# A megakernel's reload of queries and keys: the transfer begun by ScalarE instead of SyncE

## What is computed

```python
h = _L0_tok_ref(x, ln1_g, ln1_b, W, b, ln2_g, ln2_b)      # layernorm, patches @ W + b, layernorm
h = jnp.concatenate([h, txt], axis=1)
h = h + _L0_attn_ref(_layernorm(h), Wq, bq, Wk, bk, Wv, bv, Wo, bo)
h = h + _L0_ffn_ref(_layernorm(h), W_r, W_k, W_v, mu_r, mu_k)

# _L0_attn_ref: heads of 16 features; n, s, e = x.shape
Q, K, V = proj(Wq, bq), proj(Wk, bk), proj(Wv, bv)         # (n, 16, s, 16)
scores = jnp.einsum('nqhd,nkhd->nhqk', Q, K) * scale
out = jnp.einsum('nhql,nlhd->nqhd', softmax(scores), V).reshape(n, s, e)
```

## Time and profile before

| | |
|---|---|
| three timed runs, us | 1626.0, 1631.94, 1637.81 |
| median, us | 1631.94 |
| profiled execution: span from first to last instruction, us | 1635.7 |
| mean granted clock of TensorE | 0.968 of full speed |
| PE busy | 89% of the span |
| ACT busy | 67% |

### The profile page before, as it was taken

One profiled execution on the slowest core, in us unless ns is written; L12 is line 12 of the kernel. 1 busy time (PEld: TensorE's weight loads), 2 busy tenths in 40 slices (PEclk: granted clock), 3 DMA queues, 4 the chain that ended last, 5 costly groups with the idle time before them and its releaser, 6 DMA issues. The chain is left out here.

```text
span 1635.7 us, 53680 instructions
## 1 busy us (share of the span) xinstructions
PE 1454.6 (89%) x18762; PEld 1382.2 (85%) x18762; DVE 1332.3 (81%) x3075; ACT 1099.9 (67%) x2230; POOL 973.6 (60%) x1507
## 2 busy tenths in 40 slices
PE   4678899899999999999999999999999999998856
PEld 4677898898998898889898898998988988897756
DVE  5576888798988989898898888898898988888642
ACT  4455777677777776776777676777777776775543
POOL 2121566567656666666766765675675676576556
PEclk8798999999999999999999999999999999999988
DMA  4279979889877887888887896898898799887651
GB/s 121 59 141 138 141 147 150 125 159 157 143 157 141 147 155 143 150 137 165 149 140 157 151 141 127 167 157 141 152 154 140 151 159 140 156 151 118 131 74 37
DMA packets 702658, 227.65 MB, mean 139 GB/s; under 512 B 617470, under 2 KB 673854, under 8 KB 702394
## 3 DMA queue, kind: packets, MB, share of 16 engines
q1 hardware_dynamic: 702394, 224.23, 77.9%
HBM read 121.64 MB, written 89.64 MB: 129 GB/s over the span
## 5 line engine op out<-in xcount | busy, mean ns | idle before, releaser
L1026 PE MATMUL bank<-wqkv,xnT 128*126 128x384 f32 (+1 forms) x1728 | 354.2, 349 | 5.5 <-issue 5.5
L1118 PE MATMUL bank<-wtok,xT 128*98 128x258 f32 x2304 | 310.2, 290 | 12.0 <-DVE xT L770 11.4
L1026 PEld LDWEIGHTS bank<-wqkv,xnT 128*126 128x126 f32 (+1 forms) x1728 | 294.0, 185 | 18.3 <-issue 10.2
L1118 PEld LDWEIGHTS bank<-wtok,xT 128*98 128x98 f32 x2304 | 294.2, 171 | 14.6 <-DVE xT L770 13.2
L667 POOL TENSOR_TENSOR mixp<-mixf,mixp 128x364 fp32r<-128x364 f32 x192 | 185.2, 976 | 107.2 <-ACT mixp L1000 106.6
L921 ACT ACTIVATE arena<-qk,ymask 128x768 f32<-128x768 f32 x192 | 164.0, 926 | 97.6 <-DMA qk<-qkv_dram 97.6
L843 DVE TENSOR_TENSOR qkvt<-bank,bqkv 126x384 f32<-126x384 f32 (+1 forms) x288 | 154.0, 548 | 48.5 <-PE bank L1026 47.0
L654 POOL TENSOR_TENSOR dT<-zT 128x364 f32<-128x364 f32 x96 | 79.7, 851 | 153.9 <-ACT zT L994 153.9
L609 POOL TENSOR_TENSOR rs<-ve,small 126x3 f32<-126x3 f32 (+1 forms) x160 | 150.3, 940 | 12.5
L607 POOL TENSOR_TENSOR ve<-mv,small 126x3 f32<-126x3 f32 (+1 forms) x160 | 58.8, 368 | 158.8 <-DVE mv L865 104.0
L765 DVE TENSOR_REDUCE xs<-xim 84x14 f32<-84x1792 f32 x64 | 128.7, 2011 | 23.1 <-ACT xim L955 22.8
(11 more groups left out here) (121 smaller groups left out, 3339.6 us busy)
## 6 DMA issues: line engine op xcount, KB each, us to landing
xim<-in_x SPq DMA_DIRECT2D x128, 294.0 KB
qk<-qkv_dram SPq DMA_DIRECT2D x48, 768.0 KB, 8.3
qkv_dram<-qkvt SPq DMA_DIRECT2D x96, 378.0 KB
arena<-qkv_dram SPq DMA_DIRECT2D x384, 48.0 KB, 3.9
qkv_dram<-qkvt SPq DMA_DIRECT2D x48, 336.0 KB
o_dram<-probs SPq DMA_DIRECT2D x288, 48.0 KB, 1.9
out<-h SPq DMA_DIRECT2D x96, 126.0 KB
on<-o_dram SPq DMA_DIRECT2D x64, 126.0 KB
```

Of the source, the lines that this page charges most:

```text
L1026: ins = mm(psum, left(a, k), right(b, k), start=t == 0, stop=t == len(terms) - 1)
L1118: ins = mm(place("tok", c)[0:PT, 0:E + 2], xT[:, a, i0:i0 + GRID // 2, :].rearrange("p i w -> p (i w)"), wtok[:, b, ch, :], start=t == 0, ...
```

## The change

The step `qk_in` leaves SP's program and comes into ACT's, at the same place of the order (15678), ahead of `kspread` in the loop over the steps. Source, target, semaphores and waits are the same.

```diff
@@ SP's program
-                    for k in due(q, s, "qk_in", 0):
-                        after_all(qkv_out, q, k)
-                        after(kb_sb, q, k - 1, 4)
-                        after(q_sb, q, k - 1, 2)
-                        src = qkv_dram[k % CPQ, :, :, 0:2 * HD]
-                        qk_in.done(sp.dma_start(qk[:, :, :], src.rearrange("(g t) i j -> (t i) g j", t=8)))
@@ ACT's program
                     for n in weights_due(q, s):
                         square_weight(n)
+                    for k in due(q, s, "qk_in", 0):
+                        qkv_out.wait(act, q, k)
+                        settle(act)
+                        kb_sb.wait(act, q, k - 1, 4)
+                        settle(act)
+                        q_sb.wait(act, q, k - 1, 2)
+                        src = qkv_dram[k % CPQ, :, :, 0:2 * HD]
+                        qk_in.done(act.dma_start(qk[:, :, :], src.rearrange("(g t) i j -> (t i) g j", t=8)))
                     for yy in range(4):
                         for k in due(q, s, "kspread", yy):
```

## The result

| | before | after |
|---|---|---|
| median of 4 timed runs, us | 1633.84 | 1799.58 |
| lowest to highest, us | 1626.0 to 1637.81 | 1797.34 to 1801.17 |
| profiled span, us | 1635.7 | 1795.3 |
| mean granted clock of TensorE | 0.968 | 0.933 |

The kernel became 10.2% slower, ratio 1.1022 [1.099, 1.1055]. The forecast was 1651 us with a range up to 1696: the sign was right, the size 166 us instead of 19, and the result lies above the range.

A forecast was written before the change was run, and what follows sets the result against it. PE was taken to bound the kernel, busy 1454.6 of 1635.7 us, with at most 43.8 us to win before the scores. Terms of +8, -8 and +19 us gave 1651 us (+1.2%), range 1608 to 1696.

The forecast's parts named there:

- When ACT can issue: At ACT's new place: ACT comes before qkv_out lands and stands 1.1, 2.9, 1.3 us in third, first, second chunk.
- Term 1: ACT's wait delays mixh and xn, costing PE 0.5 us in each quad's third chunk: +8 us, bounds 0 to 32.
- Term 2: Earlier copies in the second chunk remove PE's idle before the scores: -8 us, bounds 0 to -43.8.
- Term 3: On its own queue qk shares DMA engines with xim and v_in; third chunk lands later: +19 us.
- lower end: Third chunk: of 0 to 3.1 us reaching PE, 1.2 was taken, giving 19 us.
- upper end: Third chunk: landing up to 729, with 3.1 us reaching PE, 50 us in place of 19.
- Shared descriptor generator: Rival: ACT and SP share one generator, so ACT's early issue delays o_in: 66 us, 1698 us; chance 0.14.
- Faster: Rival: transfer keeps its speed, ACT's holds fall into idle time, scores come earlier: 27 us, 1605 us; chance 0.20.
- no change: Rival: Term 1 and Term 2 as forecast, Term 3 nothing, as qk hardly notices sharing: 1632 us; chance 0.24.
- signs that the prediction asked for: Waits and landings to check: qk landing 9 to 10 us says Term 3, 8 or less says Faster.
- PE's waits before `on`: unchanged: Sign at PE's transposes of on: unchanged from 29.0 us in the forecast, doubled or more if the generator is shared.

The follow-up runs named there:

- e3: Kernel before, SP still issuing the transfer, with ACT also waiting for qkv_out at the place where the changed kernel does: 1633.92 us, ratio 0.998.
- e1: Changed kernel, with SP holding the v_in transfers until the chunk's qk transfer has landed: 1712.25 us, ratio 1.0451.
- e12: Kernel before, with an extra transfer of 4096 pieces of 32 bytes right ahead of qk in the same queue: 1779.05 us, ratio 1.0908.
- e13: Kernel before, with the qk transfer bringing only 32 of 48 groups from the second chunk on: 1589.11 us, ratio 0.9744.
- e5: e1, with the load beside a quad's third qk transfer also waiting until that has landed: 1704.79 us, ratio 1.0453.
- e2: Changed kernel, with SP waiting at the step's old place until the qk transfer has landed: 1738.88 us, ratio 1.0616.
- e7: Kernel before, one queue, with SP waiting right behind the qk transfer until it has landed: 1710.87 us, ratio 1.0496.
- e9: Changed kernel, with o_out moved behind the next chunk's last qkv_out in SP's order: 1846.76 us, ratio 1.1317.

## Why the prediction was right or wrong

**When ACT can issue: right.** Forecast were holds of 1.1, 2.9 and 1.3 us in third, first and second chunk. The time line of ACT has 2.98 in the first chunk (above), 1.12 in the third and 1.47 in the second:

```profile
786.51 0.37 ACTq L917 DMA_DIRECT2D qk<-qkv_dram  x1
786.98 0.91 ACT L1002 ACTIVATE mixp<-mixf 128x364 fp32r<-128x364 f32 x2 [1.12 <-DMA qkv_dram<-qkvt]
...
855.54 0.57 ACT L953 ACTIVATE xT<-bank 128x420 fp32r<-128x420 f32 x1 [1.47 <-DMA qkv_dram<-qkvt]
```

The issue took 0.37 us, where 0.39 was assumed. All holds together are 57.3 + 24.1 = 81.4 us in the waits after; 5.3 x 16 = 85 were worked out.

**Term 1, the hold's price of 8 us: measured as nothing** by e3 (0.998 [0.9943, 1.0017]), in its bounds. **Term 2, -8 us: the earlier issue came** (4.40 to 3.15 us on the mean from the last `qkv_out`), and was swallowed by the landing.

**Term 3, the second queue, +19 us: here it failed.** The mechanism was named, its size was far too small. The sum allowed 19 us. Measured were 4.17 us of landing in each of 48 chunks, 200 us, of which the earlier issue gave 60 back. Three steps of the working led there.

1. *Only the third chunk was priced.* The prediction took 1.2 us in 16 chunks. In the first it let the earlier issue be "eaten", in the second it took the landing as it was. But `v_in` follows the transfer in all three. Landings grew by 4.5, 2.7 and 5.2 us. e1 is the test: one wait for `v_in` gives back 87 of 166 us, and the landings then are 11.1, 8.9 and 11.3.
2. *The lower end was chosen.* For `v_in` stood "0 to 3.5 us more", and the lower end was taken "because that end has a row under it". A row for contention between queues could not exist in a trace with one queue; the absence was read as evidence. The third chunk's landing came at 13.3 us, by the upper end 13.1 (729 less 715.9).
3. *A shift was priced once, where it goes round.* Of 4 us the prediction let up to 3.1 "reach PE", after subtracting cover, and it wrote that "SP catches up every chunk, where it waits for DVE before `o_out`". That wait (37 chunks of 48) isn't slack that takes up a shift, it is the place where the ring closes: DVE's `probs` come from the very transfer, and the last `qkv_out` of the next chunk is behind it in SP's order. A late landing makes the next issue late. e12 shows it with the queue and ACT left alone: 2.4 us put in, 2.8 us of period lost. e13 shows it backwards, as far as PE lets it.

Had the three landings been right and the ring been seen, the sum would have been 48 x (4.1 - 1.25) = 137 us, with 4.1 as the mean of 4.5, 2.7 and 5.2. The rest up to 166 lies in the rest of the ring (0.69 us a chunk, some 33 us). Of these 0.69 us the scores alone, slower at a lower granted clock, have 0.38 (1.77 to 2.15 us on the mean; last section). The remainder no run separates.

**Rivals.** *Shared descriptor generator*: 1698 us would have been nearer the measured time, but the hold that it priced isn't there. (In its price stands "less the idle time before the scores, 2.6"; 3.7 less the 0.58 of that row is 3.1, which makes 74 us and not 66.) SP's DMA behind the old place took 0.75 us for two transfers, beginning 1.6 us after ACT's issue of 786.51, where the kernel before needed 4.80:

```profile
788.15 0.75 SPq L477 DMA_DIRECT2D xim<-in_x  x2
```

SP isn't wholly untouched, though. Its eight issues of `v_in`, which begin some 5 us after ACT's issue, took 9.3 us on the mean of chunks 5 to 42, against 6.0 before and 4.6 in e1, where they come behind the landing. Whether SP is held there in making the pieces or by full queues no run separates. SP catches up: it waits for `probs` in all 48 chunks.

*Faster* and *no change* fell with the landing. The signs that the prediction asked for pointed at term 3 (a landing of 9 to 10 was to say so: it was 12.9), except that "PE's waits before `on`: unchanged" did not hold, 29.0 to 50.3.

The Trainium skill (DMA: Bandwidth & Descriptors, Queues, rings and completion order) says that a DMA engine takes turns between queues that have work. The prediction worked out by it that the third chunk would come at the upper end, 50 us in place of 19. On the landing this trace agrees, 13.3 us. On the turns it doesn't agree with the prediction's reading, one piece of 128 bytes against one of 7168: the page lets an engine drain a whole packet of several descriptors at a turn, and this trace has 19 pieces of `qk` for each piece of the other queue beside `load`, and 0.51 beside `v_in` (last section). The same page (Issuing engines are not separate DMA queues) says that issuing from several engines "will only save the time on the sequencer". Here that isn't all it does: it saved 1.25 us of issue and cost 4.2 of landing a chunk, because the order that one queue had given was lost (e1, which restores a part of it by a wait, gives back 87 us).

**What stays open.** e5 and e2 have mean landings of 9.2 and 8.7 us, where it was 8.5 before, and are still 4.5% and 6.2% slower. In their traces the copies end 4.4 us after the landing on the mean, where they ended 3.5 after it before: ACT comes to them late. But e7 has the 3.5 too, and from the last `qkv_out` to the landing 0.7 us less than before, and is 5.0% slower all the same. So holding SP lengthens another path, in which PE's wait for `v_in` stands; by which steps was not tried. And no run gives the transfer its old landing on its own queue without a hold somewhere, so what the lost order costs is bounded by e1 and e12 and not measured by itself.

## What to carry to other kernels

Before pricing a shift of one instruction, look for a ring: follow the chain from it until it comes back to the same kind of instruction one iteration later, through the order of a queue as well as through data. If every step of the ring starts within a few tenths of its releaser, each microsecond counts once per iteration, and no idle time elsewhere covers it. And a single DMA queue is also a priority list: a transfer of many small pieces that moves to its own queue loses its place to everything that is issued meanwhile.

## What the runs showed of the hardware

**How the queues share.** The DMA view of the kernel after, by queue: packets, share of the 16 engines. At 788 to 790 us, with `qk` almost alone:

```profile
q10 hardware_dynamic: 2921, 0.37, 137.6%
q1 hardware_dynamic: 27, 0.02, 3.2%
```

At 791 to 793, beside `load` with its pieces of 7168 bytes:

```profile
q1 hardware_dynamic: 47, 0.26, 70.6%
q10 hardware_dynamic: 915, 0.12, 66.6%
```

The transfer moves 2921 / 2 = 1460 pieces of 128 bytes in a microsecond when alone and 915 / 2 = 457 beside the large ones, 19 for each of q1's 47. At 828 to 830, in the quad's first chunk and beside `v_in` with its pieces of 64 bytes, it gets 981 in 2 us, 490 a microsecond, while q1 gets 1921. So the transfer falls to a third of its rate alone in both cases, and the queues don't take turns piece for piece: 19 pieces of `qk` stand against one of q1 in the one case, 0.51 in the other. Before, in one queue, the stretch 719 to 723 has 5184 / 4 = 1296.

**The clock follows the idle time.** In the chunk followed above PE had idled 4.59 us before its scores, and 0.96 us in the kernel before. The stretch of the scores after, and before (us, then busy us and instructions of PE, PEld, DVE, ACT and POOL, then granted clock, DMA share and GB/s):

```profile
836.40:839.30 2.90, 2.84 (x97) 2.71 (x97) 2.00 (x6) 2.90 (x5) 0.97 (x1) 0.50 0.58 182
...
760.50:762.20 1.70, 1.65 (x97) 1.58 (x98) 1.59 (x4) 1.70 (x4) 0.50 (x1) 1.00 1.28 88
```

At a granted clock of 0.50, the lower level of 1.2 GHz, the scores took 2.81 us, at 1.00 they took 1.60. This is 1.2 of the 1.3 us by which "scores to last division" is longer in the table of the ring. In chunks 5 to 42 the scores took over 2 us 20 times after and twice before. Over the whole execution PE's work is the same in all kernels, its busy time isn't: 1444.1 us at a mean granted clock of 0.975 (e13), 1454.6 at 0.968 (before), 1479.1 at 0.948 (e1), 1501.7 at 0.933 (after), 1524.2 at 0.908 (e9). A kernel that makes PE wait pays again in PE's own work, here 47 us of 160.
